# Decoder layer with routed experts: the expert weights laid out for one long run per partition, and one expert load issued later

## The reference

```python
# 1. gated linear recurrence over the sequence
z = sigmoid(x @ Wz + bz);  h~ = x @ Wh + bh
h_t = (1 - z_t) * h_{t-1} + z_t * h~_t
x = x + sigmoid(h @ Wg + bg) * h
# 2. cross attention, 16 heads of 32, 77 keys, causal mask, then Wo, bo
# 3. mixture of experts: 4 experts, the 2 best of each token
weights = softmax(top2(x @ gate_W + gate_b))
h   = relu(layernorm(x @ W1[e] + b1[e]) * g1[e] + be1[e])
y_e = layernorm(h @ W2[e] + b2[e]) * g2[e] + be2[e]
x = x + sum over the two chosen experts of weight * y_e
```

## Time and profile before

| | us |
|---|---|
| median of 3 runs | 1229.69 |
| lowest and highest | 1224.35, 1237.48 |
| the profiled execution | 1224.35 |
| its span, first to last instruction | 1222.6 |

### The profile page before, as it was taken

One profiled execution on the slowest core, in us unless ns is written; L12 is line 12 of the kernel. 1 busy time (PEld: TensorE's weight loads), 2 busy tenths in 40 slices (PEclk: granted clock), 3 DMA queues, 4 the chain that ended last, 5 costly groups with the idle time before them and its releaser, 6 DMA issues.

```text
span 1222.6 us, 24524 instructions
## 1 busy us (share of the span) xinstructions
PE 1164.1 (95%) x6041; PEld 981.0 (80%) x6042; DVE 930.9 (76%) x2196; ACT 732.7 (60%) x2114; POOL 456.3 (37%) x410
## 2 busy tenths in 40 slices
PE   6999999999879999999999989988999999999993
PEld 5788888888758888888888877867888888888882
DVE  6888888887745777877878777777877777777774
ACT  5323333323557758677586762666787777777773
POOL 4040000000033323445344354365755555555543
PEclk9999999999979999999999999999999999999998
DMA  8754554544610112041130418888555444444433
GB/s 271 224 158 164 180 180 150 179 144 169 195 69 1 45 60 105 9 140 43 61 104 10 164 36 180 278 221 229 88 87 79 85 80 83 86 81 82 84 64 42
DMA packets 83237, 143.90 MB, mean 118 GB/s; under 512 B 20460, under 2 KB 24752, under 8 KB 82309
## 3 DMA queue, kind: packets, MB, share of 16 engines
q1 hardware_dynamic: 63872, 101.60, 25.5%
q0 software_dynamic: 18464, 39.14, 17.5%
q10 hardware_dynamic: 837, 2.41, 0.6%
HBM read 78.83 MB, written 67.83 MB: 120 GB/s over the span
## 4 chain that ended last, share of the span: by engine, by line
PE 70%; issue 9%; DVE 7%; DMA 5%; ACT 3%; POOL 2%; SPq 1%; DVEq 1%; POOLq 0%; another core or an unknown queue 0%; ACTq 0%
PE banks L1052 26%; PE banks L673 14%; PE banks L738 5%; PE banks L878 5%; PE banks L868 4%; DMA out<-rows,scatter_rows 4%; PE banks L837 3%; PE banks L854 3%; PE banks L1080 2%; PE banks L1064 2%; PE banks L894 2%; ACT rows L1265 2%; DVE operands L1489 1%; ACT operands L1144 1%; PE banks L886 1%
## 5 line engine op out<-in xcount | busy, mean ns | idle before, releaser
L1052 PE MATMUL banks<-operands 128*128 x1608 | 391.0, 398 | 14.3 <-DVE operands L1489 6.3
L1052 PEld LDWEIGHTS banks<-operands 128*128 128x128 f32 x1608 | 299.4, 190 | 78.8 <-issue 10.8
L673 PE MATMUL banks<-operands 128*128 128x512 f32 (+2 forms) x1224 | 291.1, 394 | 3.6 <-DVE operands L1489 3.6
L673 PEld LDWEIGHTS banks<-operands 128*128 128x128 f32 (+1 forms) x1224 | 226.5, 192 | 48.4 <-DVE operands L1489 3.7
L1144 ACT ACTIVATE operands<-banks 128x512 fp32r<-128x512 f32 (+3 forms) x328 | 192.4, 608 | 108.7 <-PE banks L868 43.3
L1489 DVE TENSOR_TENSOR operands<-banks,operands 128x512 fp32r<-128x512 f32 (+3 forms) x328 | 218.5, 684 | 45.7 <-ACT operands L1144 41.7
L1265 ACT ACTIVATE rows<-banks,score_shift 128x77 f32<-128x77 f32 x512 | 162.4, 372 | 29.6 <-DVE score_shift L1711 28.9
L1144 ACT ACTIVATE operands<-rows 128x512 fp32r<-128x512 f32 (+3 forms) x79 | 55.3, 709 | 164.6 <-DVE rows L1560 137.9
L1414 ACT ACTIVATE banks<-banks,param_cols 128x128 f32<-128x128 f32 x268 | 99.2, 430 | 81.4 <-PE banks L1080 80.0
L2460 POOL DMA_INDIRECT out<-rows,scatter_rows x67 | 106.6, 1591 | 110.0 <-DVE rows L2199 65.5
L2384 POOL TENSOR_TENSOR rows<-rows,score_rec 128x1232 f32<-128x1232 f32 x32 | 72.1, 2253 | 155.0 <-DVE score_rec L1719 155.0
(11 more groups left out here) (178 smaller groups left out, 1709.9 us busy)
## 6 DMA issues: line engine op xcount, KB each, us to landing
expert_parts<-operands SPq DMA_DIRECT2D x32, 512.0 KB, 3.0
operands<-expert_parts SPq DMA_DIRECT2D x8, 2048.0 KB, 10.4
rows<-in_x SPq DMA_DIRECT2D x8, 1024.0 KB, 5.5
rows<-in_L_ffn_W SPq DMA_DIRECT2D x32, 256.0 KB, 3.5
x_rows<-rows SPq DMA_DIRECT2D x8, 1024.0 KB, 4.3
rows<-x_rows SPq DMA_DIRECT2D x8, 1024.0 KB, 5.9
xf_rows<-rows SPq DMA_DIRECT2D x32, 256.0 KB, 2.4
out<-rows SPq DMA_DIRECT2D x32, 256.0 KB
```

Source lines behind the costliest of these rows:

```text
L673: last = nc.tensor.matmul(dst, stationary(a, k), moving(b, k), start=(t == 0 and k == 0), stop=(t == len(terms) - 1 and k == n_k - 1))
L1052: last = nc.tensor.matmul(dst, stationary[:, a, k, :], weights[:, w, bass.ds(e, 1), a2, k, :].rearrange("p e f -> p (e f)"), start=False, ...
```

## The change

The DRAM tensor of expert parts gets the partition ahead of part and k, so that a load reads one run of 16 KB for each partition; the stores into it still write runs of 2 KB, now 8 KB (part) and 16 KB (partition) apart. In SBUF the experts become the outer dimension: W1 and W2 of expert e lie side by side, W2 of expert 0 at units 24 to 40. That place is in use until the last output projection, so `load_expert(1)` is issued behind the wait for o3; the last two base rows of chunk 6 are stored ahead of the slot loads of pairs 3 and 4.

```diff
-        ws_d = dram("expert_parts", [2 * NE, 2, KC, P, D], F32)
+        ws_d = dram("expert_parts", [2 * NE, P, 2, KC, D], F32)
...
-        weights = r_at(8, 4 * NE * KC * D).rearrange("p (w e a k f) -> p w e a k f", e=NE, w=2, a=2, k=KC)
+        weights = r_at(8, 4 * NE * KC * D).rearrange("p (e w a k f) -> p e w a k f", e=NE, w=2, a=2, k=KC)
...
-                dst = ws_d[e2, :, kc].rearrange("a p f -> p a f") if isinstance(c, int) else ws_d[
-                    bass.ds(e2, 1), :, bass.ds(kc, 1)].rearrange("m a k p f -> p (m a k) f")
+                dst = ws_d[e2, :, :, kc, :] if isinstance(c, int) else ws_d[
+                    bass.ds(e2, 1), :, :, bass.ds(kc, 1), :].rearrange("m p a k f -> p (m a k) f")
...
-                sp.dma_start(weights[:, w, e].rearrange("p a k f -> p (a k) f").bitcast(F32),
-                             ws_d[s].rearrange("a k p f -> p (a k) f")).then_inc(w_in[s], 16)
+                sp.dma_start(weights[:, e, w].rearrange("p a k f -> p (a k f)").bitcast(F32),
+                             ws_d[s].rearrange("p a k f -> p (a k f)")).then_inc(w_in[s], 16)
...
             load_rows(b2_rows, "L0_ffn_b2", b2_in)
-            sp.wait_ge(mm_done, mm_num(last, "v3") + 1)
-            load_expert(1)
             for j in range(2, TPC):
                 store_xf(last - 1, j)
-            for j in range(2):
+            for j in range(TPC):
                 store_base(last - 1, j, slot3(last - 1)[:, j, :])
             load_slot_pairs(3, 5)
-            for j in range(2, TPC):
-                store_base(last - 1, j, slot3(last - 1)[:, j, :])
             sp.wait_ge(mm_done, mm_num(NCH, "o3") + 1)
+            load_expert(1)
...
-                            weights[:, w, bass.ds(e, 1), a2, k, :].rearrange("p e f -> p (e f)"),
+                            weights[:, bass.ds(e, 1), w, a2, k, :].rearrange("p e f -> p (e f)"),
```

## The result

| | before | after |
|---|---|---|
| median, us (20 runs each) | 1229.87 (1224.35 to 1238.31) | 1238.22 (1235.02 to 1248.12) |
| ratio of the times | | 1.0066, 95% interval 1.005 to 1.0084 |
| profiled execution, us (span) | 1224.35 (1222.6) | 1244.41 (1242.6) |
| TensorE's clock over the span | 0.984 | 0.975 |

The change makes the kernel 8.4 us slower. The two profiled executions lie 20 us apart, because that of before is the fastest of its runs and that of after nearly the slowest. Up to 11 of the 20 us go with TensorE's clock, by an estimate that takes TensorE as always busy: (1 - 0.975) x 1242.6 = 31.1 us lost in after against (1 - 0.984) x 1222.6 = 19.6 us in before.

The account below looks back on a forecast made before the run. TensorE was taken as mostly busy, losing 12.3 us in the expert stage where scatter-adds share DMA engines with expert loads. All terms came to 0: 1224.35 us profiled + 0 = 1224.4, 1229 for a median, range 1217 to 1241.

Parts of the forecast that it names:

- The stores: Stage A, 32 stores of parts in 2 KB pieces now 16 KB apart: ScalarE's waits cost the path 0.
- The scatter-adds: Expert stage, five scatter-adds beside expert loads: two opposed effects, -2.6 to +2.1 us on the path, taken as 0.
- quicker loads: Expert loads in 16 KB runs land 1.2 us sooner; three scatter-adds behind them gain 3.6 us together.
- long runs that hold others off: Two scatter-adds issued just ahead of a load come out only behind it, +6.5 us together.
- B: Rival: expert loads' long runs stall the other transfers, at 293 GB/s +10.9 us, 1240; decides from about 330 GB/s down; chance 0.13.
- the 12.3 us of the stretch: Nine tiles from 778 to 848 us take 69.49 us instead of 57.15; the loss was put down to expert loads.
- the steady tile: Last stretch of the expert stage, matmuls only: keeps 6.35 us a tile.
- the moved load: load_expert(1), expert 0's second matrix, issued near 757.4 us, needed at 774.1: margin of 6 us and more, cost 0.
- Rival C: The moved load comes too late, so tile 0's second product waits: 2 to 4 us, 1232; chance 0.05 with the late gather.
- A: Rival: long runs free the DMA queue in the expert stretch; limit all 12.3 us, 1217, with half 1223; chance 0.20.
- Three signs: Expected after: load_expert(1) issued at 756 to 759 us, tile 1's transposes near 778, nine tiles in 67 to 72 us.
- The likeliest case: Whole kernel: no net effect, -2.6 to +2.1 us around the median; 0.62 together with the rival of bytes at the same rate.

Follow-up runs that it names:

- e13: The changed kernel with two staging buffers in turn for chunks 0 to 5, so ScalarE waits for the store of two pieces ago; 1235.14 us, ratio 1.0041.
- e7: The kernel before without expert loads 3 to 7, every tile using expert 0's matrices; 1215.18 us, ratio 0.9896.
- e6: The kernel before with the change's DRAM layout plus one free 2 KB row in each partition, loads in 16 KB runs; 1235.46 us, ratio 1.0044.
- e15: e6 timed a second time, against the kernel before; 1235.0 us, ratio 1.0022.
- e18: e6 timed a third time, on one chip with e16; 1231.63 us, ratio 1.0024 to the kernel before.
- e14: The changed kernel with one free 2 KB row behind each partition's 16 KB in DRAM; 1232.59 us, ratio 1.0009 to the kernel before.
- e21: e14 again, on one chip with e19; 1232.94 us, ratio 1.0019 to the kernel before.
- e16: e6 with 64 bytes also left free behind every 2 KB row, so loads have 2 KB runs; 1227.31 us, ratio 0.9987 to the kernel before.
- e19: The changed kernel with the short padded DRAM rows of e16, loads in 2 KB runs; 1227.77 us, ratio 0.998 to the kernel before.
- e20: e16 timed again, against the kernel before; 1228.69 us, ratio 0.9984.
- e3: The kernel before with k outside the part in DRAM and SBUF: stores in 4 KB runs, loads in 16 KB runs; 1230.81 us, ratio 1.0001.
- e10: The changed kernel with k outside the part in DRAM and SBUF, as in e3; 1231.94 us, ratio 1.0011 to the kernel before.
- e11: e3 once more, for a second profile and more times; 1230.26 us, ratio 1.0007 to the kernel before.

## Why the prediction was wrong

**The stores: the step that failed.** The prediction said: "TensorE is at nine tenths or more in nearly every slice of that stage all the same, so ScalarE is ahead of it there. 0." It had the right question (what if each of the eight waits grows) and even an end to it (22 us for ScalarE, none of it for the path). Two things were wrong. That ScalarE waits with TensorE busy doesn't say by how much ScalarE is ahead: the slack was some 0.4 us in a later chunk, and the wait grew by 0.8; in the first chunk the delay also brought VectorE's four scalings to a worse moment. And the unknown cost, named as such ("No row shows stores of this pitch"), was kept out of the range of the sum. Its size: 284.0 and 284.2 us from first to last store in the two kernels with this layout, 279.3 to 279.7 in the fifteen others with one buffer and stores that don't merge: 4.5 us. e13 brings 4.0 of them back.

**The scatter-adds: a second term, mis-sized.** The prediction had two effects, quicker loads (-2.6 us) and long runs that hold others off (which takes that to +2.1, so 4.7 us), and took the middle of -2.6 and +2.1, as if the second were there by half. The runs show it whole: 4.7 +- 2.9 and 5.2 +- 2.7 us for long runs against short padded ones. The first is there in part, too. The loads' bytes ran at 421 GB/s (4.9 us, forecast 4.7). In the one pair of profiles they landed 0.5 us sooner at least and 0.3 in the median; over all profiles the mean of the medians is 9.5 us with 16 KB runs (eleven profiles) and 10.5 with 2 KB runs in one DMA (seven, without e7), so the 1.2 of the forecast was not far off. And the short padded rows, with loads at 409 GB/s, are 2.2 +- 1.5 us faster than before. Against the kernel before, which is what the change replaced, the five timings with 16 KB runs and a padded pitch (e6, e15, e18, e14, e21) are 3.3 +- 1.0 us slower (means, pooled). With the stores that makes 4.5 + 3.3 = 7.8 of the 8.4 us. In the single profile of after the scatter-adds stayed within the forecast's 7 to 10 us (6.75 to 9.98); the 10 to 11 us are in other profiles. Of the rivals B was nearest in kind, and wrong in its condition: it asked for loads under 330 GB/s, and the runs stalled the others at 421.

**Right:** 9.9 of the 12.3 us of the stretch are the late loads' doing (e7); the steady tile stays at 6.35 us; TensorE doesn't wait for the moved load (the forecast left 13.0 us from its issue to the 24 matmuls, it had 11.6); the matmul's address costs nothing. Rival C didn't come about. A didn't come about in the changed kernel, where a fifth more bandwidth (421 against 343 GB/s) came together with long runs and bought no time; with short runs nearly the same rate goes with some 2 us, far from A's 6 to 12. Three signs failed in the profile of after: `load_expert(1)` was issued at 770.9 us instead of 756 to 759 and the transposes of tile 1 began at 791 instead of near 778, since the whole passage came later, and the nine tiles took 73.95 us instead of 67 to 72. The likeliest case's range, 1226 to 1232, was missed by 6 us; the wide one held by luck: its upper end was B's, and the stores, which made over half of the loss, were not in it.

**Open.** Layouts with short rows and a padded pitch (e16, e19, e20) are 2.2 +- 1.5 us faster than the kernel before, pooled over three timings of which none alone is clear, and their loads move a fifth more bytes per us. That the one is the cause of the other was not tried by itself, nor why the places of before are read at 343 GB/s. Kernels with 4 KB stores and 16 KB loads (e3, e10, e11) are 1.5 +- 1.6 us slower than before, the padded ones 3.3 +- 1.0; the intervals meet.

## What to carry to other kernels

Where an engine waits for a buffer to be stored, the wait in the profile doesn't tell the slack: where no row gives the slack, put the cost of a longer round trip into the range. A layout that lengthens runs on the loading side is to be priced on the storing side as well, by the dimensions that SP's instruction gets and by where the pieces come to lie. Where small indirect transfers stand on the path, test the new places and the longer runs apart: here the places went with the higher rate, and the long runs gave the gain away.

## What the runs showed that was not expected

- For the same 256 pieces of 2 KB, an issue on SP takes 390 ns with two dimensions (128 and 2) in DRAM and 566 to 568 ns when they merge into one of 256; landing is 3.0 and 3.3 to 3.4 us in the median. 128 pieces of 4 KB take 352 ns and 2.8 us.
- The median hides the store that is waited for: it lands after 2.98 us before and 3.89 after.
- A 2 MB load moves at 343 GB/s in runs of 2 KB from the places of before, at 409 in runs of 2 KB from padded rows, at 421 in runs of 16 KB (611 ns a packet). A scatter-add beside it lands up to 3 us later with long runs.
- A delay of about half a microsecond moved the start of four VectorE instructions against GpSimd's DMA issues, and they took 3.27 us instead of 2.08, in three profiles of twenty, those of the three kernels whose stores are long and have one buffer.
- Two profiles of one kernel (e3, e11) gave 78.75 and 70.74 us for the same nine tiles: a stretch in which transfers collide needs several profiles, where the stores' stretch repeats to 0.4 us.
